# Graph attention on one core: two head pairs at a time, seven banks in turn, masks laid by ScalarE for four or five heads of eight

## What is computed

```python
q, k, v = (x_norm @ W + b).reshape(N, 8, 64)          # three of them
ws = einsum('ehd,ehd->eh', q[origin], k[destination]) * SCALE * edge_weights
e = exp(ws - segment_max(ws, origin)[origin])
att = e / (segment_sum(e, origin)[origin] + 1e-16)
values = segment_sum(att[:, :, None] * v[destination], origin)
values = (values @ W1 + b1) @ W2 + b2
x = x + (xn + values) + linear_attention(xn)          # xn: normalised x
x = x + digits(layernorm(x))                          # adds 0 or 2 in 32 columns
```

## Time and profile before

| | us |
|---|---|
| runs | 804.14, 804.55, 809.38; median 804.55 |
| the profiled execution | 803.23, of which its span is 801.5 |
| TensorE busy in the span | 736.1 (92%) |
| VectorE, ScalarE, GpSimd busy | 563.7, 388.2, 401.3 |
| attention: first scores to the last ffn's end | 352.7 to 791.1 |

### The profile page before, as it was taken

One profiled execution on the slowest core, in us unless ns is written; L12 is line 12 of the kernel. 1 busy time (PEld: TensorE's weight loads), 2 busy tenths in 40 slices (PEclk: granted clock), 3 DMA queues, 4 the chain that ended last, 5 costly groups with the idle time before them and its releaser, 6 DMA issues.

```text
span 801.5 us, 13739 instructions
## 1 busy us (share of the span) xinstructions
PE 736.1 (92%) x4643; PEld 446.3 (56%) x4682; DVE 563.7 (70%) x1295; ACT 388.2 (48%) x917; POOL 401.3 (50%) x399
## 2 busy tenths in 40 slices
PE   1997798898999999979999999999999999999984
PEld 0543345544445654436666666666666876667662
DVE  4468767684223252349998998999999887788696
ACT  0411110122130223117777777878788866566561
POOL 1007777777777777777777777875000000001030
PEclk9999799998999999999999999999999999999996
DMA  7779886798755588104444444435552323422203
GB/s 233 196 272 328 316 301 243 241 337 293 246 183 183 178 297 295 39 5 148 175 150 173 154 170 158 164 119 213 161 202 79 138 94 123 150 97 92 93 1 128
DMA packets 69636, 143.66 MB, mean 179 GB/s; under 512 B 22187, under 2 KB 54251, under 8 KB 65599
## 3 DMA queue, kind: packets, MB, share of 16 engines
q1 hardware_dynamic: 47084, 119.42, 41.5%
q10 hardware_dynamic: 9136, 17.39, 6.6%
q0 software_dynamic: 13344, 5.92, 4.0%
HBM read 77.99 MB, written 64.80 MB: 178 GB/s over the span
## 4 chain that ended last, share of the span: by engine, by line
PE 76%; DVE 8%; SPq 6%; DMA 4%; ACT 3%; issue 2%; ACTq 1%; another core or an unknown queue 0%; DVEq 0%
PE bank L942 16%; PE bank L1176 12%; PE bank L1139 12%; PE bank L1158 11%; PE bank L936 9%; SPq L435 5%; PE bank L1204 4%; PE bank L1149 3%; DMA V<-in_edge_attr_dram 3%; PE bank L1182 2%; PE bank L1049 2%; DVE AR L1604 2%; PE bank L1000 1%; DMA kv_rows<-AR 1%; DVE lstat L1662 1%
## 5 line engine op out<-in xcount | busy, mean ns | idle before, releaser
L536 POOL DMA_INDIRECT w_tab<-pay,idx x330 | 340.6, 1032 | 154.5 <-issue 99.9
L1139 PE MATMUL bank<-KT,QT 64*128 64x512 f32 (+1 forms) x480 | 116.4, 562 | 4.4 <-DVE AR L1593 2.5
L1176 PE MATMUL bank<-AR,V 128*64 128x128 f32 (+1 forms) x1600 | 114.4, 281 | 0.0
L795 ACT ACTIVATE AR<-AR,nmx 128x512 f32<-128x512 f32 (+1 forms) x160 | 105.7, 662 | 14.4 <-DVE nmx L1608 14.4
L936 PE MATMUL bank<-AR 128*128 128x512 f32 (+1 forms) x288 | 106.1, 527 | 4.7 <-ACT QT L667 2.8
L942 PE MATMUL bank<-AR 128*128 128x512 f32 x240 | 108.1, 606 | 2.5 <-ACT AR L723 2.5
L1604 DVE CUSTOM_DVE_ANT_0 AR<-bank,AR,MX 128x512 f32<-128x512 f32 (+1 forms) x106 | 100.9, 990 | 9.3 <-remote 4.3
L609 POOL DMA_INDIRECT AR<-kv_rows,xd x10 | 10.6, 1063 | 179.3 <-PE bank L1176 159.2
L1176 PEld LDWEIGHTS bank<-AR,V 128*64 128x64 f32 (+1 forms) x1600 | 85.2, 137 | 20.6 <-issue 20.6
L803 ACT ACTIVATE bank<-AR 128x512 f32<-128x512 bf16 (+1 forms) x89 | 49.0, 551 | 78.0 <-DVE MX L1604 76.9
L936 PEld LDWEIGHTS bank<-AR 128*128 128x128 f32 x288 | 54.5, 192 | 51.6 <-issue 45.9
(11 more groups left out here) (267 smaller groups left out, 974.7 us busy)
## 6 DMA issues: line engine op xcount, KB each, us to landing
w_tab<-ztile SPq DMA_DIRECT2D x20, 2280.0 KB, 14.5
AR<-w_tab SPq DMA_DIRECT2D x20, 2048.0 KB
AR<-w_tab SPq DMA_DIRECT2D x10, 1344.0 KB
w_tab<-ztile SPq DMA_DIRECT2D x3, 1800.0 KB, 13.6
w_tab<-pay,idx POOLq DMA_INDIRECT x330
w_tab<-ztile SPq DMA_DIRECT2D x2, 1700.0 KB, 8.8
...
```

The source lines that it names most:

```text
L536: pool.indirect_dma_start(out=w_tab, out_offset=bass.IndirectOffsetOnAxis(ap=idx[:, k, j:j + 1], axis=0), in_=pay[:, k % RING, j, :], in_o ...
L795: act.activation(ws[u % 3][hh][:, 0:n], ws[u % 3][hh][:, 0:n], ACT.Exp, bias=nmx[:, u % 4, hh:hh + 1], accum_out=DG[g][:, c, 2 * p + hh:2 ...
L1139: last = mm(bs[hh][:, 0:m], qs[hh], KT[64 * hh:64 * hh + 64, p, d0:d0 + m], start=not over, stop=over and g < 2, skip_group_check=over)
L1176: last = mm(bank[4 + w % 2][64 * hh:64 * hh + 64, p * P:(p + 1) * P], v, PT[u % 2][hh][0:rws, i * P:(i + 1) * P], start=(i == 0), stop=(i ...
```

## The change

The unit of the loops becomes `d`, two units (four heads); `q = d % 2`, so that a tile has an even and an odd step. TensorE runs for each d: the four heads' scores, then those masks that TensorE still adds, then in turn inverse (even steps), factor, ffn and loser_k (odd steps), then the transposes of step d-1 and the values of step d-2. Seven banks are used in one rotation for everything but the sums of values, which have bank 7 alone (`USES` lists all uses in TensorE's order, and each bank has a semaphore that counts its reads). `ws` has four sets and `PT` four. The masks of four heads of eight (five in group 2) are laid by ScalarE, from unit 6 on. ScalarE and VectorE have new orders; ffn and inverse come one tile later than before; `bits` is split into `centred`, `gains` and `bits`, and all of the digit part stands at VectorE's end. GpSimd's third gather of losers (c = 2) waits for the end of group 1, since its buffer now holds a `ws` set until then.

```diff
-SB = (0, 1, 6)
+ND = NU // 2
+NB = 7
+ODD_ON_ACT = ((2,), (1, 2), ())
+OVER_MASK = (((3, 1), (1, 1), (2, 0), (2, 1)), ((3, 1), (1, 1), (2, 0), (2, 1)), ((2, 0), (2, 1), (3, 1), (0, 0), (1, 0)))
...
-    return u // 4 >= NT and u % 4 in (0, 1)
-def laid(u):
-    return u >= 2 and u % 4 != 0
-def laid_before(u):
-    return sum(laid(i) for i in range(u))
+    return u % 4 in ODD_ON_ACT[u // 4 // NT]
+def laid(u, hh):
+    return u > 5 and (u % 4, hh) in OVER_MASK[u // 4 // NT]
+def lay_order(d):
+    late = d // 2 >= 2 * NT
+    if d % 2:
+        order = ((1, 0), (0, 0), (0, 1), (1, 1))
+    else:
+        order = ((0, 0), (0, 1), (1, 1)) if late else ((1, 1), (0, 0), (0, 1))
+    return [(2 * d + 2 + i, hh) for i, hh in order if d + 1 < ND and laid(2 * d + 2 + i, hh)]
...
+USES = []
+for _d in range(ND + 4):
+    _w, _q = _d // 2, _d % 2
+    if _d < ND:
+        USES += [("s",) + x for x in four(_d)]
+    if _q == 0 and 2 * NT <= _w - 2 < NW - 1:
+        USES += [("r", _w - 2)]
+    if _q == 1 and NT <= _w - 1 < NW:
+        USES += [("f", _w - 1)]
+    if _d == ND + 1:
+        USES += [("r", NW - 1)]
+    if _q == 1 and 2 * NT <= _w - 2 < NW:
+        USES += [("y", _w - 2)]
+    if _q == 1 and 2 * NT <= _w + 1 < NW:
+        USES += [("l", _w + 1)]
+    if 1 <= _d <= ND:
+        USES += [("t",) + x for x in four(_d - 1)]
+USE_OF = {what: i for i, what in enumerate(USES)}
...
+        def use(what):
+            return bank[USE_OF[what] % NB][:, :]
+        def read(what):
+            return s_bk[USE_OF[what] % NB]
+        def free(eng, what):
+            r = USE_OF[what]
+            if r >= NB:
+                eng.wait_ge(s_bk[r % NB], r // NB)
+        def gone(eng, what):
+            r = USE_OF[what]
+            eng.wait_ge(s_bk[r % NB], r // NB + 1)
...
+                if c == 2:
+                    pool.wait_ge(s_pv, 4 * 2 * NT)
...
+            def lay_mask(u, hh):
                 w = u // 4
                 n = GROUPS[w // NT][1]
                 act.wait_ge(s_pen, w + 1)
+                free(act, ("s", u, hh))
+                act.activation(use(("s", u, hh))[:, 0:n], pen[w % 2][:, 0:n], ACT.Copy).then_inc(s_laid, 1)
...
+            for d in range(ND):
+                w, q = d // 2, d % 2
+                late = w >= 2 * NT
+                if q == 0:
+                    if late:
+                        pairs(2 * d - 2)
+                    if NT <= w - 1:
+                        change(w - 1)
+                    if 2 <= w <= NT + 1:
+                        keep(w - 2)
+                    if d >= 1 and not late:
+                        pairs(2 * d - 2)
+                    for u, hh in lay_order(d):
+                        lay_mask(u, hh)
+                    if d >= 1:
+                        pairs(2 * d - 1)
+                    exps(2 * d)
+                    exps(2 * d + 1)
+                else:
+                    if 2 * NT <= w - 1:
+                        inverse(w - 1)
+                    if 2 * NT <= w + 1 < NW:
+                        loser_k(w + 1)
+                    pairs(2 * d - 2)
+                    if not late:
+                        pairs(2 * d - 1)
+                    for u, hh in lay_order(d):
+                        if hh == 0:
+                            lay_mask(u, hh)
+                    if late:
+                        pairs(2 * d - 1)
+                    exps(2 * d)
+                    for u, hh in lay_order(d):
+                        if hh == 1:
+                            lay_mask(u, hh)
+                    exps(2 * d + 1)
+            change(NW - 1)
+            root(0)
+            pairs(NU - 2)
+            pairs(NU - 1)
+            inverse(NW - 1)
+            root(1)
+            normed()
...
+            def scores(d):
+                w, q = d // 2, d % 2
+                m = min(n, N - d0)
+                if g == 2 and q == 0:
+                    gone(pe, ("l", w))
+                for p in (2 * q, 2 * q + 1):
+                    u = 4 * w + p
+                    over = [laid(u, hh) for hh in range(2)]
+                    bs = [use(("s", u, hh)) for hh in range(2)]
+                    qs = [QT[64 * hh:64 * hh + 64, p, c * P:(c + 1) * P] for hh in range(2)]
+                    for hh in range(2):
+                        if over[hh]:
+                            pe.wait_ge(s_laid, LAID_OF[u, hh] + 1)
+                        else:
+                            free(pe, ("s", u, hh))
+                    for hh in range(2):
+                        last = mm(bs[hh][:, 0:m], qs[hh], KT[64 * hh:64 * hh + 64, p, d0:d0 + m], start=not over[hh], stop=over[hh] and g < 2, skip_group_check=over[hh])
+                        if over[hh] and g < 2:
+                            last.then_inc(s_s[2 * (p % 2) + hh], 1)
+                    if g == 2:
+                        for hh in range(2):
+                            last = mm(bs[hh][:, m:n], qs[hh], KTx[w % 2][64 * hh:64 * hh + 64, p, :], start=False, stop=over[hh], skip_group_check=over[hh])
+                            if over[hh]:
+                                last.then_inc(s_s[2 * (p % 2) + hh], 1)
+                if q == 0:
...
+            def transposes(d):
+                g = d // 2 // NT
+                for u, hh in four(d):
                     pe.wait_ge(s_exp, 2 * u + hh + 1)
+                    free(pe, ("t", u, hh))
+                    bl = blocks(g)
+                    for i, (a, rws, _) in enumerate(bl):
+                        last = mm(use(("t", u, hh))[0:rws, i * P:(i + 1) * P], ws[g][u % 4][hh][:, a:a + rws], ident[:, :],
+                                  start=(i == 0), stop=(i == len(bl) - 1), is_transpose=True)
                     last.then_inc(s_t, 1)
...
+            for d in range(ND + 4):
+                w, q = d // 2, d % 2
+                if d < ND:
+                    scores(d)
+                if q == 0 and 2 * NT <= w - 2 < NW - 1:
+                    inverse(w - 2)
+                if q == 1 and NT <= w - 1 < NW:
+                if d == ND + 1:
+                    values(NU - 2)
+                    values(NU - 1)
+                    inverse(NW - 1)
+                if q == 1 and 2 * NT <= w - 2 < NW:
+                    ffn(w - 2)
+                if q == 1 and 2 * NT <= w + 1 < NW:
+                    loser_k(w + 1)
+                if 1 <= d <= ND:
+                    transposes(d - 1)
+                if 2 <= d <= ND:
+                    values(2 * d - 4)
+                    values(2 * d - 3)
...
+            for d in range(ND):
+                w, q = d // 2, d % 2
+                if q == 0:
+                    late = w > 2 * NT
+                    if NT <= w - 1:
+                        change(w - 1)
+                    if NT <= w - 2:
+                        merged(w - 2)
+                    weighted(2 * d, 0)
+                    weighted(2 * d, 1)
+                    if d >= 1 and not late:
+                        odd_of(2 * d - 2)
+                    weighted(2 * d + 1, 0)
+                    if not late:
+                        shift_of(2 * d)
+                    weighted(2 * d + 1, 1)
+                    if d >= 1 and not late:
+                        odd_of(2 * d - 1)
+                    if late:
+                        shift_of(2 * d)
+                    shift_of(2 * d + 1)
+                    if 2 * NT <= w - 2:
+                        scaled(w - 2)
+                    if late:
+                        odd_of(2 * d - 2)
+                        odd_of(2 * d - 1)
+                    if NT <= w - 1:
+                        denominators(w - 1)
+                else:
+                    weighted(2 * d, 0)
+                    weighted(2 * d, 1)
+                    weighted(2 * d + 1, 0)
+                    shift_of(2 * d)
+                    weighted(2 * d + 1, 1)
+                    if w + 1 < NW:
+                        mask(w + 1)
+                    if NT <= w - 1:
+                        rescaled(w - 1)
+                    if 2 * NT <= w - 2:
+                        added(w - 2)
+                    shift_of(2 * d + 1)
+                    odd_of(2 * d - 2)
+                    odd_of(2 * d - 1)
+            change(NW - 1)
+            merged(NW - 2)
+            scaled(NW - 2)
+            centred(0)
+            denominators(NW - 1)
+            odd_of(NU - 2)
+            odd_of(NU - 1)
+            gains(0)
+            rescaled(NW - 1)
+            merged(NW - 1)
+            scaled(NW - 1)
+            bits(0)
+            added(NW - 2)
+            digits(0)
+            finish(0)
+            added(NW - 1)
+            centred(1)
+            gains(1)
+            bits(1)
+            digits(1)
+            finish(1)
```

302 lines of the change are left out of this document (109 added, 193 removed).

## The result

| | before | after |
|---|---|---|
| median of four runs | 805.94 | 768.84 (766.17 to 771.5) |
| the profiled execution's span | 801.5 | 764.6 |
| attention, first scores to the end of the kernel | 448.8 | 411.2 |
| a tile in group 0, 1, 2 (tiles 2 to 9, 12 to 18, 22 to 28) | 13.33, 13.92, 15.80 | 12.43, 13.02, 13.69 |

A forecast was written before the change was run, and what follows sets the result against it. TensorE's own list was taken to bound 27 of 30 tiles. Gains of 6.5, 14.3, 2.2, 1.3, 2.65 and 2.5 less 2.5, 0.3 and 3.1 gave 23.6 us off 803.23, so 780, range 772 to 794.

The forecast's parts named there:

- Scores show no such loss at their end, since the second pair takes no longer than the first.: TensorE's scores: joining two units saves nothing there, unlike transposes and values, where each removed set is worth 0.23 to 0.24.
- 14.3: Gain in us from joining two units' phases on TensorE, 60 x 0.24; bounded by nothing and 26.
- What I had named as a sign: Tile lengths that would show the forecast right: 12.6 to 12.7 in group 0, 13.2 to 13.5 in 1, 14.7 to 15.0 in 2.
- Masks and lay wait: Groups 0 and 1: fewer TensorE mask products gain 3.5 us; waiting for ScalarE's laid mask costs 2.5, between 0 and 6.
- The masks of group 2: Group 2 loses two of five mask products on TensorE, 0.15 each, a gain of 3.0 us.
- The last `added`: VectorE's end: more work behind the last `scaled` makes it 3.1 us late, with 10.4 from it to the end.
- VectorE kept up: Rival that VectorE becomes the bound, groups 1 and 2 keeping most of their time: 793 us, chance 0.10.
- the ring of laid mask, scores and weighted pass: Rival: the mutual waits of ScalarE, VectorE and TensorE set the step, making it slower, 821 us at 8.0 a step; chance 0.05.
- the inverse's wait: Group 2: the inverse's turn, one tile later and behind scores, loses its 0.20 to 0.28 delay, a gain of 2.2 us.
- the tail's two waits: End of the kernel: waits of 1.81 and 0.84 go, since tile 28's ffn lies over the last rescaling, 2.65 us.
- The clock rival: Rival: sixteen transposes in a row lower the clock; one step in ten at 1.2 GHz adds 41 us, 821; chance 0.02.
- the estimate from the pages: Drain of TensorE at each change of array shape: 180 removed changes x 0.053 = 9.6 us.

The follow-up runs named there:

- e2: e4 with each unit's mask products directly behind its own scores on TensorE; attention 423.7 us against e4's 410.5.
- e4: Changed kernel with mask (2,1) of groups 0 and 1 added by TensorE, not laid by ScalarE; attention 410.5 us against 411.2.
- e6: e4 with five mask products a tile left on TensorE in group 2, as before the change; 768.2 us, 0.954 of before.
- e7: e4 with the first eight rows' normalisation at the end moved from GpSimd to ScalarE; 766.3 us, 0.953 of before.
- e11: The changed kernel, unaltered, run again beside other runs on one chip; 767.6 us, 0.951 of before.
- e3: Changed kernel with the masks laid as before the change (first heads of units 1, 2 and 3); attention 436.3 us against 411.2.
- e8: e7 with mask (0,1) also laid by ScalarE in group 2, six heads of eight; 776.7 us, 0.966 of before.
- e9: e4 with the second unit's mask products between the transposes of the two units; 791.6 us, 0.982 of before.
- e10: e4 with the turn of the factor ahead of the odd step's scores; 822.6 us, 1.013 of before.
- e5: e2 with transposes and values per unit too, so that every phase is per unit; 795.8 us, 0.989 of before.

## Why the prediction was wrong

**The step that failed: "Scores show no such loss at their end, since the second pair takes no longer than the first."** Scores of a unit are two pairs, 0.53 and 0.52. I compared them with each other and took equal for free. But the first holds the change into 64 rows and the second the change out of it; a pair between others takes 0.43. I had worked out that rate, and the 26 us it would give, and then took 14.3 because the switch between heads and banks inside the transposes costs nothing. That argues that the loss isn't in the banks, and doesn't say that scores have none. All times below 773, where the shorter scores would lead, got a chance of 0.04. e2 put it at 0.20 for the scores and 0.30 with the masks. From the record starts of all the borders: out of a shape 0.094 each time (0.52 against 0.43, and twice 0.20 against 0.11), into scores 0.10, into values 0.055, into mask products 0.01; one round of three is 0.44, or 0.148 a change. 60 rounds fewer are 26.6, not 14.3: **12.3 us** of the miss.

**A part that the sum had no term for.** The turns and ffn had a change of shape of their own between values and scores, and I moved them at their old 0.59 and 3.65. In group 2 the turn of the losers' rows (`loser_k`), the inverse and the factor cost 0.15 less each and ffn 0.19: 0.64 a tile, 5.8 in nine, and the factor 0.15 in ten tiles of group 1, 1.5. With them the tiles come out: 13.33 - 6 x 0.148 = 12.44 (e4 12.45), 13.92 - 7 x 0.148 = 12.88 (12.89), and 15.80 - 10 x 0.148 - 2 x 0.15 for the masks - 0.28 for the late inverse = 13.74 (13.70). What I had named as a sign, 12.6 to 12.7, 13.2 to 13.5 and 14.7 to 15.0, was missed in each group, and by most in group 2, where both terms meet.

**What was too high.** Of the 12.3 + 5.8 + 1.5 = 19.6 us, 6.3 were given back elsewhere, since the span is 13.3 under the 777.9 of my sum. Masks and lay wait: I had 3.5 less 2.5 for groups 0 and 1, and by e4 it is a loss of 0.7; that is 1.7. The wait at the lay exists where I put it, at the second head of the odd step, but is 0.33 a tile in group 1 instead of 0.2 and some 0.2 in group 0 instead of 0.05, since the even step's scores are held up inside as well. The masks of group 2 were worth 0.13 each by e6, not 0.15. The last `added` was 3.7 late instead of 3.1, partly since bits(0) took 4.2 instead of 3.8: all of it now lies beside GpSimd's passes, which e7 shows to slow it. Tiles 0 and 1 got 1.9 shorter, where 2 x 0.89 for the joining less 0.44 for masks leaves 0.6 for the start instead of 1.3, and the first scores came 0.6 later (which is scatter: in e11, the same kernel, they start at 350.8, in the profiled run at 353.4). The third gather cost 0.6 instead of 0.3, and the scores of the first tile of group 1 wait 0.8 once for VectorE. That is 4.7 of the 6.3, and the masks of group 2 would be some 0.4 more; the rest I can't place.

**What was right.** TensorE stayed the bound, VectorE kept up (12.2 of 13.1 a tile in group 1), and the ring of laid mask, scores and weighted pass did not take over. How near such waits stand show e3 and e8 (a lay that comes late), e9 (a mask product that VectorE waits for) and e10 (a bank): they lose 10 to 53 us of the attention. Transposes 1.84, values 1.90, the inverse's wait gone, the tail's two waits gone and the last ffns at 3.5 each, and 10.5 from the last `added` to the end, all as written. The clock rival did not come: with sixteen transposes in a row the granted clock is 1.00 through the three stretches of the attention.

The prediction had put the page's drain of the array against the rows. The Trainium skill, TensorEngine Tiling (Array Packing), section Key Properties, says that a change of mode drains TensorE and a change of tile within a mode does not. These traces agree with the first half as far as a cost at each change goes (e2, e5). With the second half agree the two heads side by side, which take turns between two tiles of one mode at an unbroken 0.11 a pair of values. The cost is 0.148 a change here, where the estimate from the pages was 0.053; whether it is a drain no run shows.
